# A macaron block on one core: a second buffer for the halves of h, a third slot for those of q and k, and a new order of the work

## The reference

```python
x = x + 0.5 * ffn(layernorm(x), w_gate, w_up, w_down)
x = x + attn(layernorm(x), Wq, Wk, Wv, Wproj, ...)
x = x + 0.5 * ffn(layernorm(x), w_gate, w_up, w_down)

# ffn: fp4_linear rounds each block of 16 inputs (and weights) to scale * {0, .5, 1, 1.5, 2, 3, 4, 6}
h = silu(fp4_linear(x, w_gate)) * fp4_linear(x, w_up)        # 704 wide
return fp4_linear(h, w_down)

# attn: 16 half-heads of 16 for q and k, 8 heads of 32 for v, causal
q, k = rotary(rmsnorm(q)), rotary(rmsnorm(k))
a = softmax(mask(q @ k.T / 4))
out = (a[first] - lam * a[second]) @ v
return (layernorm(out) * (1 - LAMBDA_INIT)) @ Wproj.T
```

## Time and profile before

| | us |
|---|---|
| median of 3 runs | 2306.23 |
| lowest, highest | 2303.53, 2308.92 |
| the profiled execution | 2308.14 |
| its span, first to last instruction | 2306.3 |
| PE busy | 1928.3 (84%) |
| DVE busy | 1771.7 (77%) |
| ACT busy | 1655.5 (72%) |
| POOL busy | 1421.2 (62%) |

### The profile page before, as it was taken

The page is one execution under the profiler, slowest core; times in us unless marked ns, Lnnn a source line. Parts: engine busy times, 40 slices in busy tenths (PEclk is TensorE's granted clock), DMA queues, the critical chain, the costliest instruction groups (busy, mean ns, idle before and its releaser), DMA issues. The chain is left out here.

```text
span 2306.3 us, 39555 instructions
## 1 busy us (share of the span) xinstructions
PE 1928.3 (84%) x13634; PEld 782.4 (34%) x13634; DVE 1771.7 (77%) x3817; ACT 1655.5 (72%) x2438; POOL 1421.2 (62%) x1410
## 2 busy tenths in 40 slices
PE   2577888889988889899988889898988888998955
PEld 1233333233323333333423333333333333432212
DVE  8798777868757898789876887878886988876234
ACT  3444688777887767778797676787888667788842
POOL 3777766556646676576765676666665666663313
PEclk9788899999999999999999998999999999999987
DMA  3133433223324243242243242233234224231102
GB/s 99 34 55 70 80 65 66 52 57 51 59 47 68 43 84 56 56 89 49 51 79 57 47 85 53 53 67 76 45 71 76 43 43 85 55 70 35 35 10 44
DMA packets 477493, 136.18 MB, mean 59 GB/s; under 512 B 458222, under 2 KB 477038, under 8 KB 477294
## 3 DMA queue, kind: packets, MB, share of 16 engines
q1 hardware_dynamic: 477294, 133.65, 31.1%
HBM read 11.96 MB, written 8.39 MB: 9 GB/s over the span
## 5 line engine op out<-in xcount | busy, mean ns | idle before, releaser
L1206 ACT ACTIVATE probs<-psum_s 128x1024 f32<-128x1024 f32 (+3 forms) x1280 | 1069.5, 899 | 147.9 <-PE psum_s L1516 119.9
L1534 PE MATMUL psum_o<-probs,v_sb 128*32 128x512 f32 (+3 forms) x5120 | 588.4, 548 | 31.1 <-POOL probs L1114 18.9
L1477 PE MATMUL shared<-w_gu_T,xT 128*128 128x480 f16 (+1 forms) x2304 | 519.6, 375 | 105.3 <-DMA xT<-x 50.4
L1516 PE MATMUL psum_s<-q_stack,k_stack 64*128 64x512 f16 (+3 forms) x2560 | 398.9, 357 | 122.7 <-ACT probs L1206 109.4
L1477 PEld LDWEIGHTS shared<-w_gu_T,xT 128*128 128x128 f16 x2304 | 215.6, 100 | 391.7 <-issue 110.2
L1490 PE MATMUL shared<-w_down_T,hT 128*128 128x256 f16 x2176 | 275.1, 283 | 35.6 <-DVE hq L1313 17.5
L1128 ACT ACTIVATE hq<-shared,tanh_scale 128x240 f32<-128x240 f32 (+1 forms) x384 | 172.5, 455 | 176.4 <-PE shared L1477 173.2
L1516 PEld LDWEIGHTS psum_s<-q_stack,k_stack 64*128 64x128 f16 x2560 | 96.6, 94 | 550.0 <-ACT probs L1206 439.5
L1114 POOL TENSOR_SCALAR_AFFINE_SELECT probs<-probs 128x512 f32<-128x512 f32 x256 | 180.5, 710 | 137.8 <-ACT probs L1206 136.6
L1082 POOL TENSOR_TENSOR hq<-grid,qscale 128x704 f32<-128x704 f32 x128 | 184.7, 1443 | 108.1 <-DVE grid L1330 108.1
L1490 PEld LDWEIGHTS shared<-w_down_T,hT 128*128 128x128 f16 x2176 | 212.3, 101 | 110.1 <-issue 36.2
(11 more groups left out here) (136 smaller groups left out, 2376.4 us busy)
## 6 DMA issues: line engine op xcount, KB each, us to landing
xb<-L_attn_x SPq DMA_DIRECT2D x16, 512.0 KB, 4.2
out<-xb SPq DMA_DIRECT2D x16, 512.0 KB, 3.0
xT<-x SPq DMA_TRANSPOSE x128, 3.1
hT<-h SPq DMA_TRANSPOSE x128, 3.5
k_stack<-st_k SPq DMA_TRANSPOSE x64, 3.3
q_stack<-st_q SPq DMA_TRANSPOSE x64, 3.3
k_stack<-L_ffn_w_down SPq DMA_DIRECT2D x1, 704.0 KB, 4.0
k_stack<-L_ffn_w_gate SPq DMA_DIRECT2D x1, 480.0 KB, 5.7
```

Of the source, the lines that this page charges most:

```text
L1206: nc.scalar.activation(probs[:, s % 3, 2 * u:2 * u + 2, q0:CHUNK], psum_s[u][:, :, q0:CHUNK], ACT.Exp, scale=HD ** -0.5 / QK_SCALE ** 2).t ...
L1477: last = nc.tensor.matmul(bank(e)[:, 0:2 * (hi - lo)], xs[:, x, t % 2, k, :], w_gu_T[:, w, k, 2 * lo:2 * hi], start=n == 0, stop=n == len( ...
L1516: last = nc.tensor.matmul(psum_s[u][:, j, q0:CHUNK], k_stack[half, at, h, kt % NTC * P:(kt % NTC + 1) * P], q_stack[half, c % 2, h, q0:CHU ...
L1534: last = nc.tensor.matmul(psum_o[at:at + VD, q0:CHUNK], v_sb[:, kt // NTC % SLOTS * NTC + kt % NTC, 2 * g + u, :], probs[:, s % 3, 2 * u + ...
```

## The change

Four things are changed together; what is computed and the number of instructions of each kind are the same.

1. `H16` goes from 1 to 2: `high_h` waits for the DMA of the tile of h two back.
2. `ST` goes from 2 to 3: `high_qk` waits for the DMAs of the tile three back. The wait of the first scores of a chunk is rewritten for a number of slots that doesn't divide four.
3. The planner counts a port that DVE and POOL share. For the stages named in `PORT`, on whichever of the two engines, a stage is made longer until the other engine's stage of this kind is over. `COST` has lower numbers for the stages that were waiting there on average.
4. `DUE` and `nudge` are fitted anew.

```diff
-DUE = dict(lead=72, spans=(475, 3875, 191, 418, 3643, 102925, 31, 10078, 376, 10384, 35, 352, 1329, 3205, 23, 1870),
...
-ST = 2
+DUE = dict(lead=152, spans=(761, 6602, 285, 6877, 9694, 2744475, 6, 515535, 670, 14898, 8, 13821, 2288, 1917, 6, 1004442),
...
+ST = 3
...
-H16 = 1
+H16 = 2
...
-COST = dict(add_down=0.46, add_out=0.46, copy_o=0.67, dequant_h=1.44, dequant_x=1.18, divide_h=1.45,
-            divide_x=1.24, down=1.97, gate=0.82, grid_h=1.1, grid_x=0.74, head_stats=2.75, heads_out=3.14,
-            hidden=1.29, high_h=0.79, high_qk=1.16, high_x=0.63, low_h=1.61, low_qk=2.59, low_x=1.19,
-            mask=0.73, norm_heads=0.92, norm_qk=0.99, norm_x=1.44, points_h=1.23, points_x=0.74,
...
+COST = dict(add_down=0.46, add_out=0.47, copy_o=0.68, dequant_h=1.38, dequant_x=1.06, divide_h=1.39,
+            divide_x=1.06, down=1.97, gate=0.82, grid_h=0.88, grid_x=0.68, head_stats=2.75, heads_out=3.11,
+            hidden=1.29, high_h=0.79, high_qk=1.15, high_x=0.64, low_h=1.52, low_qk=2.28, low_x=1.16,
+            mask=0.63, norm_a=1.09, norm_heads=0.68, norm_qk=0.69, norm_x=0.78, points_h=0.89, points_x=0.69,
...
+PORT = dict(grid_h=0, points_h=0, norm_qk=0, norm_heads=0, norm_x=0, quant_x=0.81,
+            divide_x=0, dequant_x=0, low_x=0, divide_h=0, dequant_h=0, low_h=0, rope_add=0, low_qk=0, mask=0)
+PORT_LEAD = 0.14
...
+            if name[0] in PORT and engine in held:
+                lock = PORT[name[0]] or weight
+                if engine == "vector":
+                    until = held["part"] if start < held["part"] else held["gpsimd"]
+                else:
+                    until = held["vector"]
+                extra = max(0.0, until - start - PORT_LEAD)
+                held[engine] = start + extra + lock
+                if engine == "gpsimd":
+                    held["part"] = start + extra + (lock / 2 if name[0] == "low_qk" else lock)
+                weight += extra
...
-                                    pe.wait_ge(turned[i], 32 * (NTC // ST) * (c + 1))
+                                    pe.wait_ge(turned[i], 32 * ((NTC * (c + 1) - 1 - i) // ST + 1))
```

25 lines of the change are left out of this document (14 added, 11 removed).

## The result

The changed kernel took 2326.40 us (median of 4 runs, 2322.79 to 2332.91) against 2304.88 us for the kernel before measured beside it (2303.53 to 2308.92). The ratio is 1.0096, with a 95% interval of 1.0077 to 1.0116. The change made the kernel slower by about 22 us; forecast was a gain of 20, and the time lies above the range too. The profiled execution took 2322.97 us with a span of 2321.2.

The account below looks back on a forecast made before the run. PE was taken as the bound, with many small stops made by whichever engine was late. The terms -9 - 1.5 - 12 + 2 = -20.5 us took the median of 2306.23 to 2286 us, range 2262 to 2320.

Parts of the forecast that it names:

- Part A: Third slot of q and k: ACT's waits for these DMAs and three long PE stops shrink, 9 us won, bounds 0 and 17.4.
- Part B: End of the program, second buffer of h: 2.7 us earlier, less 1.1 us for low_x; net 1.5 us won.
- Part C: Port of DVE and POOL counted in the plan: a third of 136 us excess goes, 12 us won, bounds 0 and 35.
- Part D: New order of PE: 16 more attention steps without other work cost 2 us, bounds 0 and 9.
- The slower rival: Copies of q and k bunch ahead of exps on ACT, 24 us lost, time 2320; chance 0.19 for above 2309.
- The waits only move: Rival: a stop that goes is followed by the next, port part 0, slots' gain halved, 2302 us; chance 0.17.

Follow-up runs that it names:

- frozen: Order of the kernel before, word for word on every engine, with the changed kernel's buffers (H16 = 2, ST = 3): 0.9964 of the kernel before.
- mix_half7: Order of before with the new buffers, the new order only in the first 36 of 64 attention steps of chunk 7: 1.0030 of before.
- experiment 4: Pieces of PE's other work moved one attention step into steps without any: 44 and 80 in frozen (0.9966, 0.9978), 39 in the changed kernel (1.0094).
- experiment 2: Changed kernel with eight transfers moved ahead at five places of SP's queue, nothing else: 1.0109 of before, against the changed kernel's 1.0096.
- mix_a4f: New buffers throughout, the new order up to the first scores of chunk 4 and the order of before behind it: 0.9971 of before.
- spread44: frozen with 44 pieces of PE's other work moved by one attention step, into steps that held none: 0.9966 of before.

## Why the prediction was wrong

**What bounds the kernel** was read rightly, but for one thing. The differences came out of PE's idle time in the attention, and out of its busy time too, which the prediction took as fixed: 11.4 us more in three batches, at a lower clock.

**Part A held**: forecast -9 us, the slots alone measured -8 (0.9966). ACT's wait for them fell from 17.4 to 6.8 us, under the 8 named, and the three long stops are gone.

**Part B held in the trace**, where 2 us go at the end, with no wait of ACT for hT there, and is too small for the ratios. Its working did not quite hold: frozen, whose end has the order of before, takes 86.7 us as well, so neither the moves of place 3 nor the 1.1 us set against them show.

**Part C failed, and in its mechanism.** The step was "the new one sees each collision and can put other work there", with a third of 136 us to go. The means named as its test were 1130 ns for `points` and 650 for the normalisation; they came out as 1256 and 822. The third mark nearly came, PE's waits for `gate` and `mask` down by a fifth (44.5 to 35.6 us) where a quarter was named; the time did not follow, since other waits rose. The Trainium skill's page "SBUF — State Buffer" (section "Who interferes with whom") calls that port an exclusive lock, held for the whole instruction; the prediction drew from it that the locked times add up whatever the order, and that with C at 0 the sum is 2297.7. The runs agree in the main: every trace has 133 to 150 us of it, and none lost a third. That the buffers alone gave 0.9964 x 2306.2 = 2298, near that 2297.7, is luck: the sum has D at +2, which frozen hasn't. I had that sentence and took the third all the same.

**Part D failed as a way to price an order.** It took one feature of the new order that could be counted, priced it at 2 us, at most 9, and held that for the whole of what 1.3% of the time depends on. Its mark, more than 200 pieces of idle time behind exps, came true with 226. But 15 us were lost with one such step more (mix_half7), moving work between the scores won nothing (experiment 4), and the order lost 30 us, more than three times the bound of 9. This is the term that failed most: +2 in the sum, +30 measured. Put into the sum: A and B -8, C 0, the order +30, together +22, which is what was measured; the +30 is the difference of two measured ratios, so this adds up by construction. The prediction's last sentence had it, "an order that the plan likes and the chip doesn't", with the rising waits for x's DMA (7.3 to 17.7 us) as its mark, though experiment 2 shows that these waits are not what was lost; it should have been a rival with a price and a large chance. Between two fitted orders no row of the trace of before gives the sign, and, in hindsight, 25 to 30 us either way would have been a fair bound for it.

**The slower rival** came near the time (2320) by another mechanism. PE's wait behind exps is 112.8 us, not over the 120 that it named. Against frozen, which has the same buffers, it is 14.7 us more, about half of what the attention is longer by. But during PE's idle time that an exp ended, ACT spent 13.3 us in instructions other than exps, against 9.4 in frozen, and of these 4.1 against 1.5 in copies of q and k: what shows directly of copies ahead of exps is 3 us, not 24. How much later the exps started behind such copies isn't measured, so this rival is made unlikely and not excluded. *The waits only move* was right of C, and of experiment 2.

In the order shown above as place 2 of before, the last row should read 32x384 instead of 32x512 (the trace has it at 1298.63 us); nothing was worked out from it.

What stays open is which moves inside the new table make the loss. Stops of 0.8 to 2.5 us behind three engines and the DMAs, and a lower clock, add up to it; repairing the largest of one kind (experiment 2) won nothing. The fastest orders measured are the old one with the third slot (0.9966) or with both buffers (0.9964), which beat both kernels and can't be told from each other, from mix_a4f or from spread44.

## What to carry to other kernels

Split a change of resources from the refit that comes with it: keep the old order word for word on the new buffers and time that first. Here it was a line of constants, it won 8 us, and it would have shown that the refitted order costs 30. An order fitted for one set of planner rules can't be judged by a better rule or by one feature counted from it; join two orders at places where both have done the same work, and the chip says which stretch is worth keeping. And a stop that ends with a late transfer is worth its length only if nobody else needs that queue then.

## What the runs showed of the hardware

TensorE's clock took a share that I had in no term. Behind a stretch with PE busy for 3.00 of 5.00 us the granted clock was 0.50 for 6.8 us, and the same matmuls took 0.43 us each instead of 0.22 (mix_half7). In the second batch, with PE's idle time up by 8.6 us (541.3 - 476.5 against 524.3 - 468.1), its busy time rose by another 8.4 us for the same instructions; the clock was 0.50 for 41.0 us of that batch, against 20.5 in frozen. Ahead of the attention, where PE idles for a third of the time, a lower clock cost next to nothing: from 60 us to the first exp the changed kernel had PE busy for 112.5 us at 0.90, and mix_a4f, with the same order there, for 119.0 at 0.86, in stretches of 176.4 and 176.8 us.

The time that DVE loses beside POOL depends little on the order: 133 to 150 us, in sum, in twenty traces of sixteen orders of the same instructions.
